# Cross-attention and quantised FFN on one core: values and output product by halves of the rows

## What is computed

```python
x = x + xattn(layernorm(x), ctx)          # ctx: 64 batches of 77 rows
x = x + ffn(layernorm(x), weight, bias)

# xattn: 16 query heads of 32, in 4 groups that share 4 key/value heads
qh = rope(q @ Wq); kh = rope(kv @ Wk); vh = kv @ Wv
attn = softmax(qh @ kh.T / sqrt(32)); out = (attn @ vh).mean(axis=heads) @ Wo

# ffn: weights cut to -1, 0, 1; inputs rounded with one scale over ALL of x
w_scale = mean(|weight|); q_weight = sign(weight) * (|weight| > 0.5 * w_scale)
i_scale = max(|x|) / 127; out = round(x / i_scale) @ q_weight.T * w_scale * i_scale + bias
```

## Time and profile before

| | |
|---|---|
| median of 3 runs | 1268.39 us (1267.43 to 1268.77) |
| profiled execution, its own time | 1268.9 us |
| span of the profiled execution | 1267.0 us |
| busy share of the span: PE, DVE, ACT, POOL | 95%, 89%, 79%, 63% |
| attention phase in the span | about 100 to 920 us |
| chain that ended last | DVE 44%, PE 35%, issue 15% |

### The profile page before, as it was taken

The page is one execution under the profiler, slowest core; times in us unless marked ns, Lnnn a source line. Parts: engine busy times, 40 slices in busy tenths (PEclk is TensorE's granted clock), DMA queues, the critical chain, the costliest instruction groups (busy, mean ns, idle before and its releaser), DMA issues.

```text
span 1267.0 us, 42077 instructions
## 1 busy us (share of the span) xinstructions
PE 1201.2 (95%) x12408; PEld 983.0 (78%) x12471; DVE 1124.7 (89%) x2410; ACT 1001.1 (79%) x2339; POOL 794.2 (63%) x1536
## 2 busy tenths in 40 slices
PE   7999999999999999999999999999789999999997
PEld 7998888888888888888888888888645555555554
DVE  4656999999999999999999999999878888888887
ACT  4566888888888888888888888888768888888886
POOL 4767898898998988989989889899700000000000
PEclk9999999999999999999999999999889999999999
DMA  9772555555555555555555543323029999999945
GB/s 291 225 205 66 160 178 169 173 173 170 164 178 166 178 168 175 170 174 162 182 163 181 164 123 94 87 84 84 2 99 398 403 396 398 399 408 396 395 206 212
DMA packets 97241, 260.26 MB, mean 205 GB/s; under 512 B 42538, under 2 KB 53994, under 8 KB 76723
## 3 DMA queue, kind: packets, MB, share of 16 engines
q1 hardware_dynamic: 97154, 259.75, 59.6%
q10 hardware_dynamic: 48, 0.07, 0.0%
HBM read 137.11 MB, written 122.64 MB: 205 GB/s over the span
## 4 chain that ended last, share of the span: by engine, by line
DVE 44%; PE 35%; issue 15%; DVEq 3%; ACT 1%; POOL 1%; DMA 0%; SPq 0%; POOLq 0%; ACTq 0%
DVE amax L903 10%; PE pT_ps L1265 10%; PE sc_ps L1265 9%; DVE x_sb L940 8%; DVE mx_sb L918 7%; DVE bn_sb L930 6%; DVE e_sb L922 6%; PE qo_ps L1069 5%; PE xT_ps L1256 5%; DVE bn_sb L910 3%; PE sc_ps L1263 2%; DVE mv_sb L947 2%; DVE rinv_sb L890 2%; PE xT_ps L1058 1%; PE pT_ps L1263 1%
## 5 line engine op out<-in xcount | busy, mean ns | idle before, releaser
L1210 PE MATMUL qo_ps<-wqs,xT_sb 128*128 128x128 f32 x2048 | 262.6, 281 | 0.9 <-ACT xT_sb L700 0.9
L1210 PEld LDWEIGHTS qo_ps<-wqs,xT_sb 128*128 128x128 f32 x2048 | 238.2, 191 | 21.5 <-issue 20.0
L1233 PEld LDWEIGHTS pT_ps<-v_blk,pT_sb 103*128 103x128 f32 x1536 | 197.3, 190 | 11.8 <-ACT pT_sb L712 0.9
L940 DVE SCALAR_TENSOR_TENSOR x_sb<-x_sb,mv_sb,xT_ps 128x512 f32 (+1 forms) x256 | 180.0, 745 | 25.5 <-DVE bn_sb L930 10.8
L1233 PE MATMUL pT_ps<-v_blk,pT_sb 103*128 103x136 f32 x1536 | 200.1, 280 | 0.3 <-ACT pT_sb L712 0.3
L1008 DVE TENSOR_TENSOR x_sb<-x_sb 128x512 f32 (+1 forms) x256 | 164.7, 684 | 1.2 <-ACT x_sb L758 1.2
L700 ACT ACTIVATE xT_sb<-xT_ps 128x512 f32<-128x512 f32 x256 | 139.1, 595 | 33.3 <-PE xT_ps L1136 28.9
L663 ACT ACTIVATE sq_sb<-x_sb 128x512 bf16 (+1 forms) x256 | 162.4, 634 | 0.6 <-DVE x_sb L940 0.2
L903 DVE TENSOR_REDUCE amax<-x_sb (+1 forms) x128 | 154.6, 1208 | 0.3 <-issue 0.3
L758 ACT ACTIVATE x_sb<-pT_ps,mean,cols 128x512 f32<-128x512 f32 x128 | 99.5, 777 | 63.6 <-PE pT_ps L1265 63.6
L1265 PE MATMUL pT_ps<-wT,x_sb 128*128 128x512 f16 x512 | 131.4, 379 | 3.2
(11 more groups left out here) (135 smaller groups left out, 2673.7 us busy)
## 6 DMA issues: line engine op xcount, KB each, us to landing
out_y<-x_sb SPq DMA_DIRECT2D x112, 1024.0 KB, 6.5
x_sb<-in_x SPq DMA_DIRECT2D x128, 512.0 KB, 3.9
x_sb<-out_y SPq DMA_DIRECT2D x48, 1024.0 KB, 8.9
x_sb<-in_ctx SPq DMA_DIRECT2D x38, 256.0 KB, 4.0
k_blk<-k_scr SPq DMA_DIRECT2D x256, 9.6 KB, 1.7
v_scr<-x_sb SPq DMA_DIRECT2D x38, 68.0 KB, 3.0
k_scr<-x_sb SPq DMA_DIRECT2D x38, 64.0 KB, 3.3
v_blk<-v_scr SPq DMA_DIRECT2D x128, 10.2 KB
```

The lines of the kernel that those rows point to most:

```text
L940: dve.scalar_tensor_tensor(out=x1_at(kj, gj, t), in0=x_sb[:, kj // 2, 2 * (kj % 2) + t, :], scalar=mv_sb[:, kj, t, 0:1], in1=bank[t][:, :] ...
L1210: last = pe.matmul(bank[2][:, t * HD:(t + 1) * HD], xT_sb[:, t, c, :], wqs[:, c, :], start=c == 0, stop=c == EC - 1)
L1233: last = pe.matmul(bank[6][:, t * HEADS * VC:(t + 1) * HEADS * VC], pT_sb[0:CR, t, c * P:(c + 1) * P], v_blk[0:CR, slot, c, :, :].rearrang ...
```

## The change

The values move to the front of the next step (from the stage VALUE to HEAD), as 12 products of 64 rows by 68 columns. For this the 77 context rows are spread over three chunks by stride 3 instead of in three runs of 103. The output product takes 32-bit operands, two products of 64 rows by 512 columns, each half of the rows into a bank of its own (`y_ps`). Values, query transposes and head transposes share `sc_ps` with the scores, and the projection lands in the first bank of `xT_ps`. The aggregation of the statistics runs one step later (ROPE). The loads of a batch's values are four DMAs instead of six. By the lines of before, PE's new order in a step is: values (1233), transposes of queries and heads, transposes of x, transposes of the probabilities, scores (1199), output product (1221), projection (1210); in it the output product and the values have left their places at the end. ACT does the exponential before it copies the projection. DVE's new order is 890, 897, 918, 922, 947, 910, 940, 903, 949, 930. POOL drops 579 and 585.

```diff
-CR = -(-SC // CHUNKS)
+HR = -(-CTX // CHUNKS)
+EP = CHUNKS * HALF
-        xT_ps, qo_ps, sc_ps, pT_ps = (
+        xT_ps, y_ps, sc_ps, pT_ps = (
+        def probs_of(slot, t):
+            return e_sb[:, slot, t, :].rearrange("p (n k) -> p n k", n=2)[:, :, 0:2 * CHUNKS * HR]\
+                .rearrange("p n (h a) -> p n h a", h=2)[:, :, :, 0:CTX]
@@ PE, in the new order @@
+                if proj:
+                    pe.wait_ge(x_in[proj[1]], proj[2] * 16 + 16)
+                if score or resid or head:
+                    at_least(pe, sub_done_t, 2 * (min(i - SCORE, NP_) if isinstance(i, int) else i - SCORE))
+                if head:
+                    pe.wait_ge(pT_copied_t, 2 * j + 2)
+                    for t in range(2):
+                        for c in range(CHUNKS):
+                            for n in range(2):
+                                rows = slice(n * HALF, (n + 1) * HALF)
+                                last = pe.matmul(sc_ps[:, n, t * 2 * VC:(t + 1) * 2 * VC],
+                                                 pT_sb[rows, t, c * P:(c + 1) * P],
+                                                 v_blk[rows, slot, c, :, :].rearrange("p h v -> p (h v)"),
+                                                 start=c == 0, stop=c == CHUNKS - 1)
+                    last.then_inc(pv_done, 1)
                 if score:
-                        last = halves(qo_ps, t * HALF, qr_sb[:, kj % 2, t * HD:(t + 1) * HD])
+                        last = halves(sc_ps, SC + t * HALF, qr_sb[:, kj % 2, t * HD:(t + 1) * HD])
                 if resid:
-                    for t in range(2):
-                        last = halves(qo_ps, P + t * HALF,
-                                      ost_sb[:, t, :, :, :].rearrange("p a b d -> p (a b d)").bitcast(F32))
+                    halves(sc_ps, SC + P, o_sb[:, :, :].rearrange("p t d -> p (t d)")).then_inc(oT_done, 1)
                 if proj:
-                        held(added_t, 2 * (j - RESID), added_count, 2)
+                        held(q_copied, j, q_count, 1)
                 if value:
-                            last = halves(pT_ps, (t * CHUNKS + c) * HALF, e_sb[:, kj % 2, t, start:start + CR])
+                            last = halves(pT_ps, (t * CHUNKS + c) * HALF, e_sb[:, kj % 2, t, c::CHUNKS])
                 if score:
-                    at_least(pe, sub_done_t, 2 * j)
+                    if head:
+                        pe.wait_ge(pv_copied, head[0] + 1)
+                    if resid:
+                        pe.wait_ge(oT_copied, resid[0] + 1)
                     pe.wait_ge(qT_copied, j + 1)
+                if resid:
+                    at_least(pe, added_t, 2 * j)
+                    for t in range(2):
+                        rows = slice(t * HALF, (t + 1) * HALF)
+                        last = pe.matmul(y_ps[:, t, :], oT_sb[rows, :], wst[rows, :], start=True, stop=True)
+                    last.then_inc(y_done, 1)
                 if proj:
-                            last = pe.matmul(bank[2][:, t * HD:(t + 1) * HD], xT_sb[:, t, c, :], wqs[:, c, :],
+                            last = pe.matmul(bank[0][:, t * HD:(t + 1) * HD], xT_sb[:, t, c, :], wqs[:, c, :],
...
@@ ACT @@
                 if head:
                     act.wait_ge(pv_done, j + 1)
+                    if score:
+                        act.wait_ge(qT_done, score[0] + 1)
+                    if resid:
+                        act.wait_ge(oT_done, resid[0] + 1)
@@ DVE @@
+                    if rope:
+                        dve.wait_ge(bn_step, 2 * rope[0] + 2)
@@ POOL @@
-                    pool.tensor_tensor(ost_sb[:, :, :, 0, :],
-                                       pw2_sb[:, :, 0, 0:D].unsqueeze(2).broadcast_to([P, 2, 2, D]),
-                                       pw2_sb[:, :, 1, 0:D].unsqueeze(2).broadcast_to([P, 2, 2, D]),
-                                       ALU.add).then_inc(o_ready, 1)
...
-                    pool.tensor_tensor(ost_sb[:, :, :, 1, :],
-                                       o_sb[:, :, 0:D].unsqueeze(2).broadcast_to([P, 2, 2, D]),
-                                       ost_sb[:, :, :, 0, :].bitcast(F32), ALU.subtract).then_inc(ost_ready, 1)
+            pool.memset(wst[:, :], 0.0).then_inc(zeroed, 1)
+            pool.memset(o_sb[:, :, :], 0.0).then_inc(zeroed, 1)
+            pool.memset(e_sb[:, :, :, :], 0.0).then_inc(zeroed, 1)
```

More of the change, by code:

```diff
@@ L63 @@
 RING = SLOTS // XS
-ZEROED = 7
+ZEROED = 10
 BR = 9
@@ L86 @@
 ROPE_BASE = 10000.0
[L89 to L97, removed]
 def build(nc, x, ctx_in, wq, wk, wv, wo, fw, fb, ident_d, qcos_d, qsin_d, kcos_d, ksin_d, out):
@@ L350, in _ @@
                 elif n == 3:
-                    for m in range(1, 4):
-                        sp.dma_start(wo4[D * m:D * m + D, :], wo).then_inc(wo_rest_in, 16)
+                    sp.dma_start(wo4[HALF:HALF + D, :], wo).then_inc(wo_rest_in, 16)
                 elif n == 5:
@@ L421, in _ @@
                         k_step(b, b)
-                    elif first < j <= first + 3:
-                        v_step(b, b, SEGS[(j - first - 1) * 2:(j - first) * 2])
+                    elif first < j <= first + 2:
+                        v_step(b, b, range((j - first - 1) * 2, (j - first) * 2))
             for n in range(ORING):
@@ L1207, in step @@
                     for t in range(2):
-                        pe.wait_ge(xT_copied_t, 2 * j + t + 1)
                         for c in range(EC):
-                            last = pe.matmul(bank[2][:, t * HD:(t + 1) * HD], xT_sb[:, t, c, :], wqs[:, c, :],
+                            last = pe.matmul(bank[0][:, t * HD:(t + 1) * HD], xT_sb[:, t, c, :], wqs[:, c, :],
                                              start=c == 0, stop=c == EC - 1)
                     last.then_inc(q_done, 1)
-                if resid:
-                    j, kj, gj = resid
-                    pe.wait_ge(oT_copied, j + 1)
-                    if not proj:
-                        pe.wait_ge(xT_copied_t, NT)
-                        pe.wait_ge(added_t, 2 * j)
-                    for t in range(2):
-                        pe.matmul(bank[t][:, :], oT_sb[:, t, :], wst[:, :], start=True, stop=True)\
-                          .then_inc(y_done_t, 1)
@@ L1223, in step @@
-                if value:
-                    j, kj, gj = value
-                    slot = kj // 2 % 2
-                    if kj % 2 == 0:
-                        pe.wait_ge(v_in[slot], gj * (2 * V_DMAS * 16) + (kj // 4 + 1) * (V_DMAS * 16))
-                    pe.wait_ge(pT_copied_t, 2 * j + 2)
-                    for t in range(2):
-                        for c in range(CHUNKS):
-                            last = pe.matmul(bank[6][:, t * HEADS * VC:(t + 1) * HEADS * VC],
-                                             pT_sb[0:CR, t, c * P:(c + 1) * P],
-                                             v_blk[0:CR, slot, c, :, :].rearrange("p h d -> p (h d)"),
-                                             start=c == 0, stop=c == CHUNKS - 1)
-                    last.then_inc(pv_done, 1)
```

195 lines of the change are left out of this document (99 added, 96 removed).

## The result

The changed kernel takes **1291.93 us** (median of 4 runs, 1291.56 to 1296.54) against 1268.05 (1267.43 to 1268.77) beside it: 1.0197 times as long, 95% interval 1.0173 to 1.022. The forecast was 1283.5, slower, in a range of 1252 to 1308. The profiled execution lasted 1292.03 us with a span of 1290.2, 23.2 longer than the span before.

The account below looks back on a forecast made before the run. The prediction took a circle of PE and ACT's copies through shared banks as the bound: 1.98, 1.34, 1.46 and 1.61 sum to 6.39, plus 0.04 is 6.43 a step; +12 for 122 steps, +3 for emptying, 1283.5 us, range 1252 to 1308.

Parts of the forecast that it names:

- The circle: PE's blocks and ACT's copies through the shared banks, load start to load start: 6.39 us summed, 6.43 a step.
- Projection to values: PE, from the projection's first load to the values' first load, with a pause of 0.09: 1.98 us.
- Scores to projection: PE, from the scores' loads through the output product (0.85) to the projection: 1.61 us.
- rival C: Output product pairs don't overlap (1388 us), or stride-3 loads take 0.2 a pair and pass the copies (1320); chance 0.08.
- Values: PE, from the values' first load to the small transposes, at the pace of 24 loads: 1.34 us.
- Handover: Small transposes to scores: transposes 0.40, to ACT 0.04, three copies 0.82, to PE's load 0.20: 1.46 us.
- Rival B: Circle as forecast but with shorter handovers: step 6.24, 1260 us; chance 0.16.
- Idle ahead of the scores: PE stands idle some 0.3 us a step ahead of the scores' loads, put down to ACT's copy of the heads.
- Sum of a step: The four terms of the circle, 6.39, plus 0.04: 6.43 us, against 6.34 on average before.
- turn of the loop: DVE's stall of 0.95 us where the loop turns, 15 times, of which 0.1 each was taken to reach PE.
- rival D: The stall at the turn of the loop stays whole, on PE's or ACT's side: +13, 1296 us; chance 0.07.
- Filling and emptying: Emptying of the pipeline, a longer chain of waits and an output product partly at half clock: +3 us, bounds 0 and 6.

Follow-up runs that it names:

- e1: The changed kernel with the probability transposes reading 128 contiguous columns instead of every third one: 1294.75 us.
- e2: The changed kernel with each value product over 34 of its 68 columns: 1295.74 us.
- e8: The changed kernel with one more DVE operation a step, the statistics of the second tile taken twice: 1295.28 us.
- e5: The changed kernel with query transposes made and copied ahead of the values, so two copies instead of three stand between values and scores: 1265.53 us.
- e3: The changed kernel with the output product as before (float32r, two times 128 rows) and the two POOL operations that feed it: 1270.81 us.
- 7: Experiment on DVE's part alone, on the kernel before: aggregation a step later 1247.82 us, DVE's whole new order as well 1222.10 us.
- e7: The kernel before with DVE's whole new order and nothing of PE's or ACT's part: 1222.10 us.

## Why the prediction was right, and where it was off

- **Sign and mechanism: right.** The circle of PE and ACT through the shared banks bounds the changed kernel. e1, e2 and e8 show that the strided loads, the columns of the values and DVE don't; e5 shows that shortening the handover shortens the step. The chain lies 96% on PE over the whole span and 1% on ACT; only in e1, where the loads don't fill the wait, does ACT stand in the chain of a step.
- **Projection to values** 1.98: 1.98 and 1.99. **Scores to projection** 1.61: 1.59 and 1.61. The output product is 1.03 to 1.05 by its records, pairs overlap (rival C's first half is out), and e3 measures its price against the old one at the 0.50 forecast in this term (0.23 in the whole step, as the terms beside it grew).
- **Values** 1.34: 1.28. The loads come 0.107 a pair apart instead of 0.112.
- **Handover** 1.46: 1.57 and 1.66, mean 1.615. This is the term that was mis-sized. The copies take 0.84 for 0.82 and the way from ACT to PE 0.07 and about 0.23 for 0.20; the start is what failed. I had 0.40 + 0.04 from PE's first load to ACT's first copy, and it is 0.66 (508.51 to 509.17) and 0.59 in the other kind of step. The last of the small transposes has its result out at 508.97 (its record starts at 508.74 and lasts 0.23), and ACT starts 0.20 behind it, where I had 0.04 from a copy that waits for one product only. In e5, with one wait less ahead of this copy, the same distance is 0.09 (509.35 to 509.44); that the number of waits is the cause is argued, not shown. Rival B had the handovers shorter than forecast; they came out longer.
- **Idle ahead of the scores**: I expected 0.3 in view, put down to the copy of the heads. After shows 0.15 in one step of two and nothing in the other. It is there (0.38 to 0.46 in e1), but strided loads and the modelled ends of the transposes cover it. The stride costs 0.18 a block of 12 (0.63 for 0.45), so the block is 0.08 longer than the 0.55 before, between the bounds of -0.18 and +0.3, and a pair takes 0.105, not the 0.2 of rival C's second half. In the change this is hidden, as I said, and becomes 17 us as soon as the handover is short.
- **Sum of a step**: 1.985 + 1.28 + 1.615 + 1.60 = 6.48, and 6.50 measured against 6.43. By terms: handover +0.155, values -0.06, the other two together within 0.01, and the 0.04 that I had added on top not found in them, which leaves 0.02 without a place. Over 122 steps it is 8.5 us more, less the 1.5 for the turn of the loop, which reached PE not at all (rival D is out): +19.2 for +12.1.
- **Filling and emptying**: 1.7 + 1.7 + 0.6 = 4 for 3. That this is so close is luck in part, since e1, e2 and e8, with the same steps, fill 2.3 to 2.8 later. The reason that I gave, more half clock, isn't borne out: the granted clock of 900 to 950 us is 0.86, for 0.80 before.
- **DVE** is 86.3% busy (258.8 of 300 us), not 91%: the operation behind the aggregation takes 0.16 for 0.44, where I took off 0.1, and the one for the second norm (line 897) 0.12 for 0.18. I had put the 0.44 down to a fresh input; by 7 it is the GpSimd operation beside it that makes it long. So engines don't meet through semaphores alone, other than the text ahead of the prediction says. The wrong size didn't matter for the time, since DVE was not the bound.
- **A reading that was wrong**: the 0.8 ns a column sets the load of a product (189 ns, 128 columns) beside that of a transpose (169, 103 columns). Among the transposes themselves 128 columns of x take 138 and 103 of the probabilities 169, so no price of a column follows. No term of the sum hangs on it.
- **What the prediction didn't see**: DVE's half of the change is worth 47 us on the kernel before. The change as a whole is this gain and a loss of 1291.9 - 1222.1 = 70 with the rest of it, of which the output product and the handover are 61 together. The remaining 9 lie mostly outside the steps, which last 5.97 with both taken back and 5.95 in e7. I had written that DVE loses a wait of 0.25 and left it there, and did not ask what that would be worth with PE's list untouched.

## What to carry to other kernels

When a change frees one full engine and reorders another, price the two halves alone: here one half was the fastest version and the other ate more than it brought. Before several results share a bank and one handover, count the copies that then stand in a row between two blocks of PE, with the start of the first, since they are paid in every step. A block of transposes ahead of a wait can hold idle time that the trace counts as busy; taking work out of the block shows it. The same holds for a short DVE operation that is long in one kernel and short in another: look at what GpSimd does beside it.

## What the runs showed of the hardware

- **Strided weight loads.** 64 rows by 128 columns of 32 bits load in 138 ns when contiguous and in 205 ns (203 in e5) with a stride of 3 numbers, and a block of 12 in pairs takes 0.45 and 0.63 us. The Trainium skill's page "SBUF — State Buffer", section Door 1: The DMA port swizzle, says of lines of 16 bytes that 32-bit data stride for free up to 4 elements, and also that at least two accesses must fall in a line for full bandwidth. By the first a stride of 3 would be free, which the trace denies; by the second it would not be, as most lines get one access, which agrees with it.
- **Value products** of 64 rows take the same mean of 276 ns by their records at 68 and at 34 columns (e2), and their pairs come 0.107 and 0.104 us apart, at the pace of the loads.
- **Mean busy share isn't need.** In e1 PE is busy 285.5 of 300 us and in the changed kernel 298.1, with the same steps.
- **A DVE operation can wait for GpSimd inside its own duration.** The operation of 128x2 numbers behind the aggregation takes 0.15 to 0.17 us with no GpSimd operation beside it (e3, before), and 0.52 on average in e7, where it always ends 0.01 to 0.04 behind the GpSimd operation that was running.
